# A pipelined language-model layer on one core: nine chunks instead of eight, the first and the last half as long, with new orders of work

## The reference

```
h = tok(x)
h = h + attn(_layernorm(h))     # RWKV block: tokens of one sequence depend on those before
h = h + ffn(_layernorm(h))      # FP4 gated layer: every token for itself
```

## Time and profile before

| what | before |
|---|---|
| median of 3 runs | 758.01 us (755.78 to 758.63) |
| the profiled execution's own time | 758.01 us |
| its span, first to last instruction | 756.1 us |
| mean granted PE clock | 0.959 |
| PE busy | 687.8 us (91%) |
| DVE busy | 589.2 us (78%) |
| ACT busy | 510.5 us (68%) |
| POOL busy | 154.3 us (20%) |

### The profile page before, as it was taken

How to read it: one execution, slowest core, us unless ns; L and a number is a source line. 1 busy time by engine, 2 the same in 40 slices (tenths; PEclk the granted TensorE clock), 3 DMA queues, 4 the chain that set the end, 5 groups by cost and what they waited for, 6 DMA issues and landing times.

```text
span 756.1 us, 9924 instructions
## 1 busy us (share of the span) xinstructions
PE 687.8 (91%) x3301; PEld 570.5 (75%) x3301; DVE 589.2 (78%) x1031; ACT 510.5 (68%) x893; POOL 154.3 (20%) x220
## 2 busy tenths in 40 slices
PE   4374799799999999999999999999999998899786
PEld 3233557698789968897889878996889777788775
DVE  0776896886988789787998698778978798773683
ACT  2663799489857896589748984789658975662231
POOL 2302500531025201530043102520152003200100
PEclk9685999899999999999999999999999999899998
DMA  4800000010002000100010000200010000000000
GB/s 126 281 2 28 28 1 2 28 29 1 14 1 70 2 1 14 43 29 1 14 43 29 1 14 2 70 1 0 15 43 1 1 14 15 0 1 15 15 0 29
DMA packets 13374, 19.34 MB, mean 26 GB/s; under 512 B 982, under 2 KB 10764, under 8 KB 13324
## 3 DMA queue, kind: packets, MB, share of 16 engines
q1 hardware_dynamic: 10720, 10.31, 4.2%
q0 software_dynamic: 2560, 8.39, 3.8%
q10 hardware_dynamic: 44, 0.01, 0.0%
HBM read 14.51 MB, written 4.19 MB: 25 GB/s over the span
## 4 chain that ended last, share of the span: by engine, by line
PE 78%; DVE 11%; ACT 4%; issue 4%; POOL 1%; DMA 1%; POOLq 0%; DVEq 0%; ACTq 0%
PE psB L557 20%; PE psC L626 16%; PE psB L584 11%; PE psC L652 10%; PE psA L548 9%; PE psA L520 6%; PE psC L640 2%; PE psA L508 2%; PE psB L530 1%; DMA rows<-L_tok_w,ids_now 1%; DVE mix L1005 1%; PE psC L612 1%; DVE scales L1160 1%; DVE mix L980 1%; PE psA L530 1%
## 5 line engine op out<-in xcount | busy, mean ns | idle before, releaser
L557 PE MATMUL psB<-cwv_s,kkT 128*128 128x256 f32 x512 | 113.2, 379 | 0.7 <-ACT kkT L838 0.7
L557 PEld LDWEIGHTS psB<-cwv_s,kkT 128*128 128x128 f32 x512 | 96.6, 190 | 16.9 <-issue 2.9
L626 PE MATMUL psC<-up_hi,xq_hi 128*128 128x352 f32 x256 | 88.6, 346 | 9.6 <-DVE xq_lo L1253 9.0
L548 PE MATMUL psA<-mix,kvr_s 128*128 128x512 f32 x192 | 89.0, 608 | 6.9 <-DVE mix L980 5.8
L652 PE MATMUL psC<-downT,hqT 128*128 128x256 f32 x384 | 86.6, 382 | 0.1
L448 POOL TENSOR_SCALAR sc_c<-mv_c 128x2 f32<-128x2 f32 x16 | 7.6, 476 | 386.6 <-DVE mv_c L1143 386.6
L626 PE MATMUL psC<-up_hi,xq_lo 128*128 128x352 f32 x256 | 84.9, 332 | 0.0
L626 PE MATMUL psC<-up_lo,xq_hi 128*128 128x352 f32 x256 | 84.9, 332 | 0.0
L652 PEld LDWEIGHTS psC<-downT,hqT 128*128 128x128 f32 x384 | 72.9, 192 | 10.5 <-ACT hqT L903 0.5
L548 PEld LDWEIGHTS psA<-mix,kvr_s 128*128 128x128 f32 x192 | 37.0, 195 | 46.0 <-issue 38.0
L980 DVE SCALAR_TENSOR_TENSOR mix<-hT,rest,mix 128x512 f32<-128x512 f32 x80 | 54.4, 747 | 16.6 <-ACT mix L754 16.6
(11 more groups left out here) (166 smaller groups left out, 1468.1 us busy)
## 6 DMA issues: line engine op xcount, KB each, us to landing
out<-h SPq DMA_DIRECT2D x16, 256.0 KB, 2.1
mix<-L_attn_cwk SPq DMA_DIRECT2D x1, 1024.0 KB, 9.4
cwv_s<-L_attn_cwv SPq DMA_DIRECT2D x1, 1024.0 KB, 12.3
hq<-L_ffn_w_gate SPq DMA_DIRECT2D x1, 704.0 KB
hq<-L_ffn_w_up SPq DMA_DIRECT2D x1, 704.0 KB, 7.1
hqT<-L_ffn_w_down SPq DMA_DIRECT2D x1, 704.0 KB, 9.7
w_s<-L_tok_w SPq DMA_DIRECT2D x1, 512.0 KB, 3.9
rows<-L_tok_w,ids_now POOLq DMA_INDIRECT x32, 4.1
```

Source lines behind the costliest of these rows:

```text
L548: mm = nc.tensor.matmul(psA[:, A.slot(f"{name}{d}")], kvr_s[:, w, k, d * P:(d + 1) * P], mix[:, w, k].rearrange("p c t -> p (c t)"), start ...
L557: mm = nc.tensor.matmul(psB[:, B.slot(name), q * D:(q + 1) * D], lhsT[:, k, (2 * j + q) * P:(2 * j + q + 1) * P], weight[:, k, :], start=( ...
L626: mm = nc.tensor.matmul(psC[:, C.slot(name), f, 0:INTER // 2], a[:, k, t * P:(t + 1) * P], b[:, w, k, f * (INTER // 2):(f + 1) * (INTER // ...
```

## The change

Nine chunks instead of eight: the first and the last hold one sequence (256 tokens, two tiles, one pair), the seven between them two. A chunk knows its width (`cs`, `tokens`, `tiles`, `pairs`) and its first tile (`tile0`). Steps for a second pair, or for tiles 2 and 3, return at once for a short chunk; operations over a whole chunk are cut to its width (their slices get `0:n`). The counts of the semaphores per chunk stay as they are: where a short chunk leaves out steps, the last one that it does increments by so much more (`last`). One wait is added: PE's c_cols of the chunk after a short one waits until d0 of the short one is emptied. SP increments the semaphore of second stores by 16 at the start, for the store that chunk 0 does not have. All five lists of ORDER are laid out anew.

```
-CHUNKS = TOKENS // CHUNK
+WIDTHS = [1] + [CS] * ((SEQS - 2) // CS) + [1]
+CHUNKS = len(WIDTHS)
...
 ORDER = {
-    "pe": [("w_turn1", 2), ("b_key1", 2), ("a_k", 1), ("b_key2", 2), ("a_v", 1), ("b_key3", 2), ("w_turn2", 2),
-        ("c_down0", 3), ("w_turn0", 1), ("a_r", 1), ("b_value0", 2), ("c_turn2", 3), ("a_turn0", 0),
-        ("b_value1", 2), ("c_turn3", 3), ("c_down1", 3), ("b_out0", 1), ("c_cols0", 2), ("b_out1", 1),
-        ("a_emb0", 0), ("c_up0", 2), ("a_turn1", 0), ("c_cols1", 2), ("b_cols", 1), ("a_emb1", 0), ("c_up1", 2),
-        ("b_gate", 1), ("c_turn0", 2), ("c_up2", 2), ("b_key0", 1), ("a_cols", 0), ("c_turn1", 2), ("w_par", -16),
-        ("c_up3", 2)],
-    "act": [("w_par", -4), ("c_sq0", 1), ("a_emb1", -1), ("c_up1", 1), ("b_high", 0), ("b_gate", 0),
-        ("c_turn0", 1), ("a_norm", -1), ("w_sq2", 0), ("c_sq1", 1), ("w_sq0", -1), ("c_up2", 1), ("a_cols", -1),
-        ("w_key", -1), ("c_turn1", 1), ("b_key0", 0), ("a_part", -1), ("c_sq2", 1), ("c_up3", 1), ("b_key1", 0),
-        ("a_k", -1), ("w_turn1", 0), ("b_key2", 0), ("a_wkv1", -1), ("a_v", -1), ("a_wkv2", -1), ("b_key3", 0),
-        ("w_turn0", -1), ("c_sq3", 1), ("a_r", -1), ("a_wkv3", -1), ("a_y", -1), ("c_turn2", 1), ("c_norm0", 0),
-        ("c_sqn0", 0), ("c_turn3", 1), ("w_turn2", 0), ("c_norm1", 0), ("c_cols0", 0), ("a_turn0", -2),
-        ("c_sqn1", 0), ("a_emb0", -2), ("w_sq1", -1), ("c_up0", 0), ("b_norm", -1), ("a_turn1", -2),
-        ("c_cols1", 0), ("b_cols", -1), ("b_part", -1)],
-    "dve": [("b_low", 3), ("c_rq1", 4), ("c_up2", 4), ("w_quant0", 2), ("w_quant2", 3), ("c_sq2", 4), ("a_mix", 2),
-        ("a_wkv1", 2), ("c_rq2", 4), ("w_key", 2), ("c_up3", 4), ("c_sq3", 4), ("w_split1", 3), ("a_wkv2", 2),
-        ("c_down0", 4), ("c_rq3", 4), ("a_wkv3", 2), ("b_value0", 3), ("c_stat0", 3), ("a_wkv4", 2), ("c_sn0", 3),
-        ("b_value1", 3), ("w_split0", 2), ("c_stat1", 3), ("c_rn0", 3), ("c_down1", 4), ("c_sn1", 3), ("b_x1", 2),
-        ("c_split0", 3), ("w_quant1", 2), ("c_rn1", 3), ("c_up0", 3), ("c_sq0", 3), ("c_split1", 3), ("b_mix", 2),
-        ("w_par", -9), ("c_rq0", 3), ("c_up1", 3), ("a_stat", 1), ("c_sq1", 3)],
-    "pool": [("b_coef", -2), ("gather0", -4), ("a_coef", -3), ("c_coef0", -2), ("c_coef1", -2), ("gather1", -4),
-        ("b_sum", -3)],
-    "sp": [("c_down1", 10), ("c_down0", 9)],
+    "pe": [("b_key3", 2), ("a_r", 1), ("w_turn2", 2), ("c_up3", 3), ("b_value0", 2), ("c_down0", 3),
+        ("c_turn2", 3), ("b_value1", 2), ("c_turn3", 3), ("w_turn0", 1), ("a_turn0", 0), ("c_down1", 3),
+        ("b_out0", 1), ("b_out1", 1), ("c_cols0", 2), ("a_emb0", 0), ("c_up0", 2), ("a_turn1", 0), ("c_cols1", 2),
+        ("b_cols", 1), ("a_emb1", 0), ("c_up1", 2), ("b_gate", 1), ("w_turn1", 1), ("b_key0", 1), ("c_turn0", 2),
+        ("a_cols", 0), ("w_par", -15), ("b_key1", 1), ("c_up2", 2), ("a_k", 0), ("b_key2", 1), ("c_turn1", 2),
+        ("a_v", 0)],
+    "act": [("w_par", -16), ("w_sq1", 0), ("a_turn1", -1), ("c_cols1", 1), ("b_cols", 0), ("b_part", 0),
+        ("a_emb1", -1), ("c_sq0", 1), ("b_high", 0), ("c_up1", 1), ("b_gate", 0), ("w_turn1", 0), ("a_norm", -1),
+        ("w_sq2", 0), ("b_key0", 0), ("a_cols", -1), ("c_turn0", 1), ("a_part", -1), ("c_sq1", 1), ("b_key1", 0),
+        ("c_up2", 1), ("a_k", -1), ("b_key2", 0), ("c_turn1", 1), ("a_wkv1", -1), ("a_v", -1), ("c_sq2", 1),
+        ("w_sq0", -1), ("a_wkv2", -1), ("b_key3", 0), ("a_r", -1), ("c_up3", 1), ("w_key", -1), ("w_turn2", 0),
+        ("a_wkv3", -1), ("c_sq3", 1), ("c_norm0", 0), ("c_turn2", 1), ("w_turn0", -1), ("c_turn3", 1), ("a_y", -1),
+        ("c_sqn0", 0), ("c_norm1", 0), ("a_turn0", -2), ("c_cols0", 0), ("c_sqn1", 0), ("a_emb0", -2),
+        ("c_up0", 0), ("b_norm", -1)],
+    "dve": [("c_sq1", 4), ("w_quant2", 3), ("a_mix", 2), ("c_rq1", 4), ("c_up2", 4), ("a_wkv1", 2), ("c_sq2", 4),
+        ("w_split1", 3), ("w_quant0", 2), ("c_rq2", 4), ("a_wkv2", 2), ("c_up3", 4), ("a_wkv3", 2), ("c_sq3", 4),
+        ("b_value0", 3), ("c_stat0", 3), ("w_key", 2), ("c_rq3", 4), ("a_wkv4", 2), ("c_down0", 4), ("c_sn0", 3),
+        ("b_value1", 3), ("c_stat1", 3), ("c_rn0", 3), ("c_down1", 4), ("w_split0", 2), ("c_sn1", 3), ("b_x1", 2),
+        ("c_split0", 3), ("c_rn1", 3), ("c_up0", 3), ("c_sq0", 3), ("w_quant1", 2), ("c_split1", 3), ("b_mix", 2),
+        ("a_stat", 1), ("w_par", -7), ("b_low", 2), ("c_rq0", 3), ("c_up1", 3)],
+    "pool": [("c_coef0", -3), ("c_coef1", -3), ("gather1", -5), ("b_sum", -4), ("b_coef", -4), ("gather0", -6),
+        ("a_coef", -5)],
+    "sp": [("c_down0", 14), ("c_down1", 13)],
 }
...
         self.base, self.parity = base, base % UNROLL
+        self.cs = WIDTHS[base] if self.exists() else CS
+        self.whole = self.cs == CS
+        self.tokens, self.tiles, self.pairs = self.cs * T, self.cs * T // P, self.cs * T // P // 2
+        self.tile0 = sum(WIDTHS[:max(base, 0)]) * T // P
...
+    def last(self, n):
+
+        return 1 if self.whole else 1 + n
...
+            sp.sem_inc(stored[1].sem, 16)
...
             def emb(j):
                 def step(ch):
+                    if j >= ch.pairs:
+                        return
                     A.wait_free(pe, ch, f"e{j}")
...
-                    mm.then_inc(a_full.sem, 1)
+                    mm.then_inc(a_full.sem, ch.last(3))
...
                     C.wait_free(pe, ch, f"q{j}")
+                    if not ch.back(1).whole:
+                        C.wait_emptied(pe, ch.back(1), "d0")
```

More of the change, by code:

```diff
@@ L443, in gather, with coefficients @@
                 return step
-            def coefficients(ch, sc, mv, coef, done=0):
+            def coefficients(ch, sc, mv, coef, done=0, extra=0):
                 n = mv.shape[1]
@@ L471, in sum_b @@
             def sum_b(ch):
                 B.wait_emptied(pool, ch, "o1")
-                for j in range(2):
+                for j in range(ch.pairs):
                     at(pool, stored[j], ch.back(2), 16)
-                nc.gpsimd.tensor_tensor(h1[:, ch.parity], h0[:], x1[:], ALU.add).then_inc(b_sum.sem, 1)
+                here = slice(0, ch.tiles)
+                nc.gpsimd.tensor_tensor(h1[:, ch.parity, here], h0[:, here], x1[:, here], ALU.add).then_inc(b_sum.sem, 1)
             def coef_b(ch):
@@ L478, in coef_b @@
                 hold(pool, b_stat, ch, 2 * TILES)
-                coefficients(ch, sc_b, mv_b, b_coef)
+                coefficients(ch, sc_b[:, :, 0:ch.tiles], mv_b[:, 0:ch.tiles], b_coef)
             def coef_c(j):
                 def step(ch):
+                    if j >= ch.pairs:
+                        return
                     hold(pool, c_stat, ch, TILES * (j + 1))
                     pair = slice(2 * j, 2 * j + 2)
-                    coefficients(ch, sc_c[:, :, pair], mv_c[:, pair], c_coef, 4 * j)
+                    coefficients(ch, sc_c[:, :, pair], mv_c[:, pair], c_coef, 4 * j, 4)
@@ L528, in columns @@
                     jobs.wait_free(pe, ch, name)
-                    for t in range(TILES):
+                    for t in range(ch.tiles):
                         mm = nc.tensor.transpose(ps(jobs.slot(name))[:, t * P:(t + 1) * P],
@@ L634, in step @@
                 def step(ch):
+                    if t >= ch.tiles:
+                        return
                     name = f"hq{t}"
@@ L729, in norm_a @@
                 at(act, wkv, ch.back(1), WKV.index("gain1") + 1)
-                for t in range(TILES):
+                for t in range(ch.tiles):
                     nc.scalar.activation(norm[:, t, :], h0[:, t, :], ACT.Identity, scale=sc_a[:, 8, t:t + 1],
-                                         bias=sc_a[:, 9, t:t + 1]).then_inc(a_norm.sem, 1)
+                                         bias=sc_a[:, 9, t:t + 1]).then_inc(a_norm.sem, ch.last(2) if t == 1 else 1)
             def y_a(ch):
@@ L736, in y_a @@
                 at(act, wkv, ch, WKV.index("numer1") + 1)
-                for t in range(TILES):
+                for t in range(ch.tiles):
                     nc.scalar.activation(y[:, t, :], h0[:, t, :], ACT.Identity, scale=sc_a[:, 1, t:t + 1],
-                                         bias=sc_a[:, 3, t:t + 1]).then_inc(a_norm.sem, 1)
+                                         bias=sc_a[:, 3, t:t + 1]).then_inc(a_norm.sem, ch.last(2) if t == 1 else 1)
             def affine(ch, dst, jobs, names, ps, g, b):
@@ L804, in norm_b @@
                 at(act, b_sum, ch, 1)
-                for t in range(TILES):
+                for t in range(ch.tiles):
                     nc.scalar.activation(x1[:, t, :], x1[:, t, :], ACT.Identity, scale=sc_b[:, 1, t:t + 1],
-                                         bias=sc_b[:, 3, t:t + 1]).then_inc(b_norm.sem, 1)
+                                         bias=sc_b[:, 3, t:t + 1]).then_inc(b_norm.sem, ch.last(2) if t == 1 else 1)
             def cols_b(ch):
@@ L909, in step @@
                     C.wait_full(act, ch, name)
-                    turned(psC, C.slot(name), hqT[:, t % 2], c_act.sem)
```

(7 more changed lines are left out.)

179 lines of the change are left out of this document (117 added, 62 removed).

## The result

The changed kernel takes 779.73 us (median of 4, 779.28 to 782.1) against 758.32 before: 1.0293 times, 95% interval 1.0259 to 1.0327. 759 was forecast, with a range up to 768. The spans of the profiled executions are 777.8 and 756.1, so 21.7 us are to be found.

What follows compares the result with a forecast made beforehand. PE's own work was taken to bound the middle, leaving only the two ends to gain. Terms 0 - 0.5 + 1.5 + 0.2 = +1.2 on 758.0 us gave 759 (no change, chance 0.38), range 748 to 768.

Steps and rivals of the forecast that it cites:

- Work of PE, +0: All matmuls: half-width chunks cost PE no extra time, key matmuls of 256 columns taking 0.117 each; upper end +4.2 us.
- Start to the first columns of C: Kernel start: out-projection at about 52 us, gate at 68, second chunk's k at 81.5, columns of stage C at 117.7.
- the lead of the first gate: Chunk 0's gate on PE: reached with 46 us lost, 9 us better than before.
- The faster rival: Second chunk's k to stage C columns: takes 28 us instead of 36, keeping the 9 us lead; 750 us, chance 0.34.
- columns at 117.7, lost 63.4 against 63.9: Second chunk's recurrence: 36 us from k to stage C's first columns, giving back the lead at the first gate.
- the head: Start up to stage C's first columns: -0.5 us in all, with ends -9 and +4.
- ACT's extra work is hidden: it is busy for 359 of 475 us: Full rounds: ACT's added work costs no time, since ACT is busy for only 359 of 475 us.
- +1.5 for five rounds: Full rounds: c_turn3 on PE may wait for c_down0 on DVE, 0.3 us in each of five; ends 0 and 2.5.
- the slower rival: Full rounds: c_turn3 waits for c_down0, standing behind a_wkv4, costing 11.5 us instead of 1.5; 769 us, chance 0.28.
- b_sum's 1 us of cover for the reversed stores: POOL's sum: waits for both stores two chunks later with about 1 us of cover; without it b_coef and b_norm are late.
- The quantising moved behind a_wkv1: First weight's quantising on DVE, formerly ahead of a_mix: takes about 3 us from before k, adds 3 between k and out.
- End, +0.2: Last rounds: 10 us lost in round 9 and 18.1 in the last half chunk, 28.3 against 28.1 before.

Runs made afterwards that it cites:

- a faster ACT: Changed kernel with c_turn0 ahead of b_key0, c_down0 ahead of a_wkv4, key squares over 64 columns only: 777.16 us; with the old store order as well, 773.83.
- the eight-chunk runs: Changed kernel's new lists with eight whole chunks: 769.98 us; the same with the first weight's quantising back ahead of a_mix: 767.24 us.
- the two fills: Kernel before with overwritten identity transposes ahead of eleven PE waits at both ends: 749.38 us; with more of them: 745.94 us.

## Why the prediction was wrong

- **Work of PE, +0:** right. The fp32r key matmuls of 256 columns start 0.117 apart, half of 0.233.
- **Start to the first columns of C:** right within 3 us. Out at 51.61 (52 forecast), gate 67.86 (68), k of the second chunk 82.16 (81.5), columns 120.69 (117.7); the lead of the first gate was given back in the second chunk's recurrence, and at the second gate the kernels stood nearly equal (+0.55). The faster rival fell with that.
- **The step that failed: "columns at 117.7, lost 63.4 against 63.9", with the head ended there at -0.5.** It ended the head at the first columns, because before the change almost nothing was lost behind them, and left out the round that the change alone has: stage C with half a chunk, A and B with whole ones. That round lost 10.9, about half of the 21.7. Its PE work (68.0) and the length that ACT and DVE need (79 to 81, with either list) could have been set against each other.
- **"ACT's extra work is hidden: it is busy for 359 of 475 us":** wrong; a mean busy share hides nothing in a chain. The forecast was +1.5 for five rounds; it was 1.07 a round. The price of the whole sum was near (40.8 against 40.0 from k to c_down0; 40.45 measured from k, 398.44, to c_turn3, 438.89), and c_turn3 did wait, for 0.25. But the slower rival had the wrong mechanism: with that wait gone the round was as long. With one table load of 1.28 taken off the way (and the old store order) the period was PE's own again.
- **b_sum's 1 us of cover for the reversed stores:** it held. In the changed kernel the sum waits for a store only in the last half chunk (4.88), with no wait of PE's columns of stage B behind it; with a faster ACT it waits for a store in either order (3.9 to 5.6).
- **The quantising moved behind a_wkv1:** both landmarks came as forecast for the short chunk, but the eight-chunk runs show that the move by itself loses 3.1 us at the first out-projection.
- **End, +0.2:** it was +6.0, of which 1.2 stands with the new lists and eight chunks as well. Round 9 went as costed (up0's wait 3.23 of 3, its 24 matmuls 5.68 of 5.70, key0's wait 2.14). The last half chunk took 48.2 from its value step to the end instead of 43.5 to 45.3: 15.8 to up0 (14.9 forecast), and the last transposes and down 10.7 instead of 7.5: 1.8 of this is more matmuls at the lower clock (8.04 against 6.21), 1.05 the wait for the second tile's copy. The forecast had taken these from rows in which PE came less idle to the same step (2.78 of wait ahead of the last transposes, not 6.25) and down had no such wait. The remaining 2 us of the end were not assigned.

Three of its small sums are off by 0.2 (16.9 + 3.3 is 20.2, 81.5 + 36 is 117.5, and the end's 10 + 18.1 is 28.1), which decides nothing. The range was too narrow since both rivals were about known waits; none was about a round that exists only after the change.

## What to carry to other kernels

When a pipeline gets one smaller item, cost the rounds in which it stands in each stage: the engine that was the bound has less to do there, while the other stages' chains are as long as before, and the difference is lost. In a round bound tightly by one engine (82.2 of 82.2), look at the length of the other engines' closed chain, table loads included, and not at their busy share. And where a tightly bound engine idles at the ends, the fill of its waits may be worth more than a new order: here it gave 1.3 to 1.5%, on the old lists.

## What the hardware showed unexpectedly

Overwritten transposes ahead of waits raise the clock of what follows: the mean granted clock rose from 0.959 of the kernel before to 0.984 and 0.995 with the two fills. At half speed in the lower level, that is 2 x (1 - clock) x span = 62, 24 and 7 us spent there, and the span fell from 756.1 to 748.2 and 744.0. The Trainium skill (TensorE: Matmul & The Clock Gate, The HAM clock gate) says that the lower clock is the default and activity lifts it; these runs agree, and in them transposes whose results nobody reads were enough to lift it.
